# One tile fewer per group of sparse chunks, and the second phase's pieces in another order on every engine

## The reference, cut to what matters

```python
x = x + delta_rule_attention(layernorm(x))     # short convolutions, 16 heads of 8, one recurrence over time
x = x + moe(layernorm(x))                      # 8 experts, the best 2 of each token count
x = x + linear_attention(layernorm(x))         # elu + 1 features, chunks with a carried state
x = x + moe(layernorm(x))                      # the same experts again

def moe(x):                                    # x: tokens x 128
    probs = softmax(x @ Wg)                    # 8 logits for each token
    topw, topi = top_k(probs, 2)
    combine = one_hot(topi) * topw / sum(topw)
    h = relu(einsum('nd,edf->enf', x, W1))     # 128 -> 256, for each expert
    y = einsum('enf,efd->end', h, W2)          # 256 -> 128
    return einsum('ne,end->nd', combine, y)
```

## Time and profile before

| What | us |
|---|---|
| median of three runs | 745.68 |
| the profiled execution, its own time | 745.4 |
| its span in the trace | 743.7 |
| PE (TensorE matmul) busy | 615.7 (83% of the span) |
| DVE (VectorE) busy | 595.9 (80%) |
| ACT (ScalarE) busy | 479.9 (65%) |
| POOL (GpSimd) busy | 470.1 (63%) |
| mean share of full TensorE clock granted | 0.933 |

### The profile page before, as it was taken

The page is one execution under the profiler, slowest core; times in us unless marked ns, Lnnn a source line. Parts: engine busy times, 40 slices in busy tenths (PEclk is TensorE's granted clock), DMA queues, the critical chain, the costliest instruction groups (busy, mean ns, idle before and its releaser), DMA issues.

```text
span 743.7 us, 17594 instructions
## 1 busy us (share of the span) xinstructions
PE 615.7 (83%) x5488; PEld 497.4 (67%) x5488; DVE 595.9 (80%) x1698; ACT 479.9 (65%) x1270; POOL 470.1 (63%) x494
## 2 busy tenths in 40 slices
PE   4826364797988979887687989989999999979797
PEld 3605142685877858766567668868887788957776
DVE  4399989999999999999988768888887888654335
ACT  3984738799797996957366648456584645563442
POOL 2017999799898998989928704425517623663534
PEclk9966667999999999999898989999999999999999
DMA  6331221303114031130020333445555645665732
GB/s 232 74 71 61 51 80 46 100 16 89 59 42 118 14 74 59 43 99 15 1 71 2 111 104 116 115 138 167 156 151 169 176 137 150 180 183 147 196 88 78
DMA packets 106767, 74.01 MB, mean 100 GB/s; under 512 B 44992, under 2 KB 94656, under 8 KB 106432
## 3 DMA queue, kind: packets, MB, share of 16 engines
q1 hardware_dynamic: 102080, 63.58, 30.3%
q0 software_dynamic: 4608, 9.45, 4.6%
HBM read 45.47 MB, written 27.53 MB: 98 GB/s over the span
## 4 chain that ended last, share of the span: by engine, by line
PE 32%; ACT 6%; DVE 3%; issue 3%; DMA 3%; SPq 2%; POOL 1%; DVEq 0%; ACTq 0%; POOLq 0%
PE bank L2139 6%; PE bank L2118 5%; PE bank L2042 4%; PE bank L2011 3%; PE bank L1874 2%; PE bank L2167 2%; ACT prod_mem L1316 2%; PE bank L2109 2%; ACT wv L1356 1%; PE bank L1846 1%; PE bank L2048 1%; POOL s_xs L961 1%; DMA hid<-in_w 1%; PE bank L1812 1%; PE bank L2062 1%
## 5 line engine op out<-in xcount | busy, mean ns | idle before, releaser
L1846 PE MATMUL bank<-w,hid 128*128 128x128 f32 x768 | 101.6, 289 | 23.7 <-DVE y_even L2730 13.3
L1846 PEld LDWEIGHTS bank<-w,hid 128*128 128x128 f32 x768 | 96.8, 203 | 33.9 <-ACT hid L1184 11.2
L893 POOL TENSOR_TENSOR oq_mem<-hist_mem,q_t 128x384 f32<-128x384 f32 (+1 forms) x96 | 101.4, 1093 | 0.0
L1184 ACT ACTIVATE hid<-bank 128x512 f32<-128x512 f32 x112 | 62.4, 594 | 36.1 <-PE bank L1826 35.5
L2139 PE MATMUL bank<-w,wv 128*128 x448 | 63.4, 285 | 11.6 <-ACT wv L1356 10.5
L2139 PEld LDWEIGHTS bank<-w,wv 128*128 128x128 f32 x448 | 55.3, 194 | 18.8 <-issue 18.3
L2598 DVE TENSOR_REDUCE hist_mem<-hist_mem 128x64 f32<-128x320 f32 x128 | 62.2, 486 | 3.4
L976 POOL DMA_INDIRECT qkv<-s_ys,back_at x32 | 30.4, 949 | 53.5 <-DMA s_ys<-q_t 28.2
L1754 PE MATMUL bank<-xnT_h,wtap_h 128*128 128x512 f32 x104 | 49.7, 478 | 15.4 <-DVE qkv L2552 6.3
L2588 DVE TENSOR_REDUCE u<-prod_mem 128x32 f32<-128x288 f32 x128 | 57.6, 450 | 3.4
L1824 PE MATMUL bank<-xT_h,w_h 128*128 128x512 f32 x112 | 50.0, 447 | 12.4 <-ACT hid L1184 12.1
(11 more groups left out here) (302 smaller groups left out, 1752.5 us busy)
## 6 DMA issues: line engine op xcount, KB each, us to landing
hid<-in_w SPq DMA_DIRECT2D x72, 128.0 KB
s_qkv<-qkv SPq DMA_DIRECT2D x24, 256.0 KB, 2.6
pin<-s_xs SPq DMA_DIRECT2D x76, 64.0 KB
pin<-s_qkv SPq DMA_DIRECT2D x16, 256.0 KB, 2.9
kk<-in_w SPq DMA_DIRECT2D x30, 128.0 KB
s_ys<-q_p SPq DMA_DIRECT2D x28, 128.0 KB, 2.8
s_ys<-q_t SPq DMA_DIRECT2D x28, 128.0 KB
s_xs<-zeros SPq DMA_DIRECT2D x40, 64.0 KB
```

The source lines that it names most:

```text
L893: tt(oq[:, :, j, :, 0:HD], s_at, bc(turned[:, n, j], 2, HD), ALU.mult).then_inc(o_part, 1)
L1184: nc.scalar.activation(hid[:, e % 2, f], bank[:, ZB + f, :], ACT.Relu).then_inc(hid_ready, 1)
L1846: last = nc.tensor.matmul(bank[:, y_bank(e, wide), tokens], hid[:, e % 2, f, tokens], w2[:, e, f], start=(f == 0), stop=(f == FC - 1))
```

## The change

`TILES` loses one tile in each group: 15 for the first, 23 for the others, 107 in all. Groups now have an odd number of tiles. A new list `PAIRS_AT` gives for each pair its group, its first tile and its width, 2 or 1. There are still 56 pairs; pairs 7, 19, 31, 43 and 55 hold one tile. Loads, turns, copies, matmuls, relus and stores of these five are half as wide. The reading of `TILES` stays safe: 2 x NT x rounds choices, spread over 8 experts, fill at most 2 x NT x rounds / 128 + 7 tiles.

The lists of pieces of the second phase are new for all five engines. No piece is added or dropped. GpSimd's list, which is short, shows how: `scatter(11)` and `scatter(12)` both stand ahead of `gather(8)`, and `lin_keep(7)` stands ahead of `scatter(14)`.

```diff
-TILES = [2 * NT * len(group) // TILE + E for group in GROUPS]
-FIRST_TILE = [sum(TILES[:g]) for g in range(len(GROUPS) + 1)]
+TILES = [2 * NT * len(group) // TILE + E - 1 for group in GROUPS]
 MOST_TILES = max(TILES)
+PAIRS_AT = [(g, first, min(2, TILES[g] - first)) for g in range(len(GROUPS)) for first in range(0, TILES[g], 2)]
...
+def loads_until(p, buffers):
+    return sum(2 * PAIRS_AT[q][2] for q in range(p % buffers, p + 1, buffers))
...
             def tile_load(p):
-                g = sum(2 * p >= first for first in FIRST_TILE[1:])
-                k = 2 * p - FIRST_TILE[g]
+                g, k, wide = PAIRS_AT[p]
...
-                for h in range(2):
+                for h in range(wide):
...
             def tile_store(p):
...
-                sp.dma_start(s_ys[g][first:first + 2 * TILE].rearrange("(h p) d -> p h d", h=2),
+                sp.dma_start(s_ys[g][first:first + TILE * wide].rearrange("(h p) d -> p h d", h=wide),
...
             gather(7)
+            lin_keep(5)
             scatter(11)
-            lin_keep(5)
+            scatter(12)
             gather(8)
-            scatter(12)
             lin_keep(6)
             scatter(13)
             gather(9)
+            lin_keep(7)
             scatter(14)
-            lin_keep(7)
...
             tile_store(40)
+            tile_store(38)
+            store_sparse(8)
+            tile_store(39)
+            store_sparse(9)
+            tile_load(44)
             tile_store(41)
-            tile_store(39)
-            tile_load(44)
...
             dense_up(6, 6)
+            dense_up(6, 7)
             dense_down(6, 5)
             dense_down(6, 6)
-            dense_up(6, 7)
             dense_down(6, 7)
```

More of the change, by code:

```diff
@@ L967, in gather @@
                 k, g = SPARSE.index(r), GROUP_OF[r]
-                last = FIRST_TILE[g + 1] // 2 - 1
+                last = max(p for p in range(PAIRS_OF) if PAIRS_AT[p][0] == g)
                 for b in range(len(ys)):
@@ L2191, in _ @@
-            lin_scores(0, 3)
-            warm(6)
-            lin_numer(0, 2)
-            lin_numer(0, 3)
-            moe_transpose(7)
+            lin_scores(0, 3)
+            lin_numer(0, 2)
+            moe_transpose(7)
+            warm(6)
+            moe_route(7)
+            lin_numer(0, 3)
+            lin_turn(1)
+            lin_project(1)
             tile_turn(0)
-            moe_route(7)
-            lin_project(1)
+            place(7)
+            tile_turn(1)
+            lin_state(0, 0)
@@ L2445, in _ @@
             tile_up(40)
+            tile_down(38)
             tile_turn(41)
+            lin_project(7)
             tile_down(39)
[L2448 removed]
             tile_turn(42)
```

832 lines of the change are left out of this document (413 added, 419 removed).

## The result

The changed kernel takes 750.42 us (median of 17 runs, 745.00 to 755.23), the kernel before 745.07 us (17 runs beside them). The ratio is 1.0069, 95% interval 1.0046 to 1.0091: slower by 5 us. The loss is 0.7%, small but clear of the noise. My forecast was 737.0 us, and 750.4 us is outside its range of 731.5 to 744.5. The profiled execution has a span of 748.6 us against 743.7 us.

What follows compares the result with a forecast made beforehand. TensorE was taken to bound 437 to 640 us, then GpSimd's three-piece chain to pair 44. 745.4 - 6.6 - 3.0 + 1.3 - 0.4 = 736.7 us, with 0.3 for the median 737.0; range 731.5 to 744.5.

Steps and rivals of the forecast that it cites:

- The five tiles: Second phase, TensorE: five tiles fewer at 1.32 us each take 6.6 us off.
- My lower end, 5.3 us: Low end of the gain from five tiles fewer, with the fourth tile's gain lost.
- The middle: 437 to 640 us: some 250 pieces reordered, net zero, with 7.4 us idle time bounding gain or loss.
- The start: Around 436 us: projection ahead of the first turn fills 1.2 us of waiting and saves 1.8 us, 3.0 in all.
- The clock's part, 1.8 us: At the start, if the clock stays up, `lin_project(1)` takes 1.98 us instead of 3.78.
- my own signs of being wrong: Middle idle well above 10 us, clock falling at the start just the same, pair 44's turn not 4 us earlier.
- GpSimd's chain: `scatter(13)`, `gather(9)`, `scatter(14)` bound pair 44; `rows(13)` moves 7.0 us, pair 44 comes 5.7 us earlier.
- The 1.3 us for `lin_keep(7)`: Loss counted because `lin_keep(7)`, now ahead of `scatter(14)`, lengthens GpSimd's chain to pair 44.
- the second rival: GpSimd keeps its time because VectorE holds `rows(13)`; pair 44 not earlier, 744.2 us, chance 0.12.
- The dense end: Last experts: `dense_up(6, 7)` ahead of `dense_down(6, 5)` removes a 0.69 us wait, of which 0.4 us is gained.
- the first rival: New TensorE gaps in the middle, 0.3 to 1 us at ten or more places, 742 us, chance 0.21.
- `store_sparse(9)` did not hold SyncE up: Rival: `store_sparse(9)`, waiting for `combine(9)`, delays SyncE ahead of pair 44's loads; 758 us, slower, chance 0.06.

Runs made afterwards that it cites:

- tiles_fill: tiles_only_b plus matmuls nobody reads: 8 identity transposes behind pair 43's up product, 16 ahead of pair 44's turn; 743.04 us, ratio 0.9979 to the kernel before.
- tiles_only_b: Changed kernel's 107-tile code with the kernel before's five engine lists: 744.27 us, ratio 0.9989; as tiles_only on the 911 us chip, 0.9949.
- order_only_b: Kernel before's 112-tile code with the changed kernel's five engine lists; 753.57 us, ratio 1.0122 to the kernel before.
- stores_early_b: Changed kernel with SyncE's stores of pairs 28 and 29 right behind that of pair 27; 745.45 us, ratio 1.0004 to the kernel before.
- both_early: Changed kernel with the moves of stores_early_b and relu_early_b together; 743.65 us, ratio 1.0003 to the kernel before.
- four_moves: both_early with lin_keep(7) behind scatter(14) on GpSimd and TensorE's dense end in the old order; 741.53 us, ratio 0.9958 to the kernel before.
- act_stores: four_moves with the stores of pairs 44 to 55 issued from ScalarE's queue instead of SyncE's; 742.56 us, ratio 0.9977 to the kernel before.
- four_fill_b: four_moves plus unread identity products, 14 ahead of tile_down(42) and 12 ahead of tile_turn(44); 743.72 us, ratio 0.9968 to the kernel before.
- five_moves: four_moves with ScalarE's lin_v(7) behind the relus of pairs 42 and 43; 743.44 us, ratio 0.9953 to the kernel before.
- relu_early_b: Changed kernel with ScalarE's relu of pair 1 ahead of the first heads of group 1; 745.65 us, ratio 1.0015 to the kernel before.

## Why the prediction was wrong

**The five tiles (-6.6 us forecast): the step that failed first.** I priced them by TensorE's busy time because TensorE was 96% busy, and took all five. Alone they gave 0.8 us, with 2.8 us less as the most that the interval allows. The 7.4 us idle of the earlier trace rows say that TensorE rarely waited, not that its partners had slack. Of three tiles' 4 us, 0.2 us was left at pair 31 (0.6 in tiles_fill): new waits for VectorE and a load took nearly half, and what took the rest is not seen. The fourth was turned into idle time and a halved clock; only the fifth gave about 1 us (tiles_only_b goes from 0.5 us behind the kernel before at pair 54 to 0.5 ahead at pair 55), and one profile is thin ground for that. My lower end, 5.3 us, was no bound at all: it should have been nothing, or a small loss.

**The middle (0 forecast): the step that cost most.** The order alone costs 9.1 us, against 1.7 + 0.4 us that I expected it to give. I read only TensorE's side of it. The 250 pieces moved within 460 to 620 us show no harm in the profile (2.1 us idle of 160, before 5.4); two moves at its ends did harm, and both are lists in which one engine's piece has been put behind others. For the stores I wrote that `tile_store(29)` stands as `tile_store(30)` did, that I leave the 12.9 us from `scatter(13)`'s start to `gather(9)`'s as they are, and that "SyncE's ten transfers fewer are nothing too, since TensorE waits for SyncE only at pair 44 and for loads of the last group". It became 18.2 us. I had asked who reads the stored data, and not who needs the buffer: the copy of pair 32 needs the one of pair 28. A load costs SyncE about 3.05 us, so five loads ahead of a store are at least 15 us, and that could have been counted from the list; with waits on the way it became 22.6 us for pair 29. The third wait, 3.0 us at pair 42, is in all eight profiles of the new order that neither fill it nor move its relu (2.9 us in order_only_b). No run took it away and left all else as it was, so its price at the end is open.

**The start (-3.0 us).** The clock's part, 1.8 us, failed: `lin_project(1)` took 3.59 us instead of 3.78, one of my own signs of being wrong. The order alone does not decide it. In the ten profiles of the new order on chips of 745 us these four matmuls took 1.98 us four times and 3.46 to 3.61 us six times, with the same pieces ahead of them. And it is worth less than 1.8 us: pair 0's copy stands at 27.0 to 27.2 us behind the scatter in three of the four (26.3 in order_only_b), at 27.5 or 27.6 in the six, against 29.4 before. What was won ahead of the first pair went into the wait for `tile_relu(1)`. With the relu in its place, 2.7 to 3.3 us are there at pair 1. That this is near my 3.0 is in part luck, since the clock's 1.8 us are not what it is made of; and the cover was not looked at.

**GpSimd's chain.** `rows(13)` moved by 6.0 us against its first phase, forecast 7.0. But the chain was misread. I took three pieces of GpSimd's for the bound of pair 44. The rows ahead of the one that I used of the earlier trace rows (658.46) are these:

```profile
656.98 0.38 ACT q_p L1363
657.38 0.38 SPq L643
657.81 0.47 SPq L643
658.46 0.78 SPq L618
```

SyncE came to pair 44 behind its own stores, which waited for ScalarE's copy of pair 41. `scatter(14)`'s landing is not on record, and GpSimd is in no piece of the chain between 600 and 712 us, before or in the changed kernel. The 1.3 us for `lin_keep(7)` have no such place in the sum either: in the changed kernel it ran from 646.95 to 648.24 us, and `scatter(14)` then waited another 3.3 us for VectorE. Nor is the 1.08 us of the earlier trace rows a wait of TensorE behind `combine(9)`: it lies between two of VectorE's operations, ahead of `combine(9)`, and TensorE worked from 675.73 to 681.6 us with no gap over 0.2. So what was to pay for the fourth tile, and 1.1 us of the second rival, were nothing.

**The dense end (-0.4 us)** had the wrong sign: +0.8 us. I looked at TensorE's last wait, and not at what the later `dense_down(6, 5)` holds up on VectorE.

**The rivals.** None was it. New gaps did come, 4.9 us more idle time from 437 to 640 us, which is the size that the first rival gave, but as two large ones and not as ten small ones. `store_sparse(9)` did not hold SyncE up: `combine(9)` began at 659.0 us, and its store was issued at 664.8, ahead of pair 44's loads at 667.4. The time also lies between my bounds for faster and slower, 738.2 and 753.1, to which I had given 0.39; 17 runs of each can tell a smaller change than that 1%. Of my signs of being wrong all three came: 12.3 us of idle time in the middle, the fallen clock, and pair 44's turn, 5.8 us later instead of 4 earlier.

**Open.** Pair 55's result stands at 289.5 to 290.7 us in five kernels (stores_early_b, both_early, four_moves, act_stores, four_fill_b) while pair 44's is anywhere from 251.4 to 256.2. It is not SyncE's stores, and not the clock at 665 us. What holds the last group there I have not found. four_moves (0.9958) and five_moves (0.9953) have the lowest ratios on chips of 745 us, are told apart from the kernel before and not from each other.

## What to carry to other kernels

A nearly full engine need not be what sets the time: here 4 us of its work gave 0.2 to 0.6 us. Before pricing work that is taken off it, look whether the engines it trades with come only just in time, and take nothing as the lower end. In lists written out by hand, check for every piece that moves back who waits for the buffer that it frees as well as for its data, how much time was to spare there, and count the time of what now stands ahead of it on its own queue. And follow a chain of waits piece by piece before naming an engine as the bound. Profiles with the same first phase start the changed part up to 5 us apart, so compare distances from the last common event.

## What the hardware showed that I had not expected

**A load that is addressed by registers costs SyncE 3.05 us for a pair of tiles.** In the changed kernel from 607.31 to 610.37 us: two register reads of 0.46 and 0.45 us, four issues of about 0.33 us with some 0.19 us around each. A store costs 0.42 to 0.47 us.

**The clock can fall behind short gaps, and not each time.** In the kernel before it was granted at 1.00 up to 436 us and at 0.50 from 438 to 442 us, and the longest gap of TensorE since 420 us was 0.82 us. With the new order it stayed at 1.00 through `lin_project(1)` in four of ten profiles.

**A copy of VectorE's that stands still beside GpSimd's addition.** L3049 (128 x 8) took 1.91, 1.91 and 1.11 us in both_early, stores_early_b and relu_early_b, where it overlaps `lin_keep(7)`, and ended as that did; in the other profiles it took 0.16 us. In the changed kernel seven other operations of VectorE ran beside `lin_keep(7)`, the reduction L2680 for instance at 0.43 us, as long as it took without it in both_early.

**Another chip, other bound.** On one chip the kernel before takes 911.0 us instead of 745. The first phase is the same there (scatter(6) at 418.9 us in tiles_only), and from about 425 us on ScalarE and VectorE stand still for up to 20 us at a time, with nothing of this core as the releaser. ScalarE in tiles_only, and GpSimd's scatter beside it:

```profile
475.19 0.59 ACT L1161 COPY xfT<-bank 128x512 f32<-128x512 f32 x1 [8.35 <-remote]
```

```profile
463.67 0.98 POOL L966 DMA_INDIRECT s_xs<-squares,row_at  x1 [0.16 <-issue]
...
472.54 0.96 POOL L966 DMA_INDIRECT s_xs<-squares,row_at  x1 [0.30 <-issue]
```

ScalarE goes on 1.7 us after GpSimd's eighth indirect DMA is issued, and the same at 568.49 us behind a gather. In the profiles of the 745 us chips no such wait is on record. Why that chip does it is not settled; four kernels ran there, and order and tiles were worth 0.6% and -0.5% there instead of 1.2% and -0.1%.
